# Second attention weights of a two-layer graph kernel: rests by two wide VectorE instructions a group, last load of x moved behind POOL's first group

## Chip, cores and metric

The kernel runs on one core of a Trainium2 chip. The metric is the device time of one execution in microseconds (us). The engines are PE (TensorE), DVE (VectorE), ACT (ScalarE), POOL (GpSimd) and SP (SyncE, which here only issues transfers).

## What is computed

The inputs are x (4096 nodes, D = 128), a weighted adjacency matrix adj (4096 x 4096) and small weights. Two layers follow each other, each added to its input:

```python
h = jnp.maximum(_layernorm(x, axis=-1), 0.0)
x = x + _L0_gnn_ref(h, adj, L0_gnn_weight, L0_gnn_bias)      # adj @ x_tangent, between norms
h = jnp.maximum(_layernorm(x, axis=-1), 0.0)
x = x + _L1_gnn_ref(h, L1_gnn_context, adj, ...)             # attention over the edges
# in _L1_gnn_ref:
logits = left[:, None] + right[None, :]
logits = jnp.where(logits >= 0, logits, 0.2 * logits)
logits = jnp.where(adj_tensor <= 0.0, -jnp.inf, logits)
coefs = jax.nn.softmax(logits, axis=-1)
return jax.nn.relu(coefs @ relation)                         # relation is h
```

A logit is a sum of a row's and a column's number, bent at zero. So the exponential of it is a product of a factor of the row and a factor of the column, with one pair of factors where the sum is negative (weights 0) and one where it is positive (weights 1). The kernel multiplies two matrices of zeros and ones (edge and negative sum, edge and positive sum) with h scaled by the columns' factors, s0 and s1.

## The kernel before, in words

**Tiling.** The 4096 rows stand in NC = 8 chunks of CH = 512 rows; the 4096 columns in NK = 32 blocks k of 128, or NC = 8 groups g of L = 4 blocks. In the first phase (until about 284 us of the trace) adj is loaded chunk by chunk, DVE turns it block by block, PE multiplies it with the tangent vectors (line 715) and ACT keeps the edges as a mask of bytes. In the second phase PE does the attention: for each chunk c and group g it runs 4 row tiles t x 4 blocks k x 2 parts, 32 matmuls of 128 x 258 (line 748, function `attend`).

**What PE multiplies.** `G[0]` and `G[1]` hold for every block k a row of GW = 258 float16 numbers: a head (h times the factor, rounded to float16), a rest (the float32 product less the head, again float16), and the factor itself as two numbers. `G[1]` is written by ACT and DVE, `G[0]` by POOL:
- ACT, `heads(g)` (line 902): four activations write the four heads of `G[1]`, each adding 1 to `head_ready`.
- DVE, `rests(g)` (line 1233): four scalar_tensor_tensor of 128 x 128, each h2 times the column `s1_col`, less the head; each adds 1 to `rest_ready`.
- POOL, the loop of lines 616 to 633: for group g three wide tensor_tensor of 128 x 512, the product with `s0_col` in float32 (line 624), the same product as a float16 head (line 625), and the rest (line 628), which adds 1 to `rest0_ready`. The float32 product is written over the h2 rows of group g - 1, so from group 1 on POOL first waits until `rest_ready` is at 4 g. Before the first group POOL waits for `weight_cols` (DVE, line 1226).

All this is done once, while chunk 0 of the attention runs. For each chunk and group DVE and ACT also make the two matrices of zeros and ones: `compare` (line 1184, two of a group's four blocks by DVE, in chunk 0's group 0 all four), ACT's signs (line 918, the other two), `part_neg` (line 1200) and `part_pos` (line 1207), which adds 1 to `parts_ready`. They have four slots, so the signs and compares of group g wait until PE has used group g - 4.

**Order of the work.** Each engine has its queue written out by hand. In chunk 0 DVE's is, for g = 0 to 7: `part_neg(g)`, `compare(g + 1)`, `rests(g)`, `part_pos(g)` (those of group 0 and the compare of group 1 stand ahead of the loop), with what is left of the first layer's last chunk in between: two sums (lines 1134 and 1138) behind group 0, and statistics (lines 1144 to 1151) behind group 3. POOL also carries pieces of the first layer's last chunk between its groups: `shrink` behind group 1 (lines 558 to 562), which ACT's tanh (line 838) waits for, ahead of its heads of group 3 and its signs of group 3; `residual` (lines 569 to 573) and `store_x1` behind group 2; `affine` behind group 4. PE starts group g of chunk 0 when `parts_ready` is at g + 1, `rest_ready` at 4 g + 4 and `rest0_ready` at g + 1.

**The loads of x.** `load_x(p)` (lines 591 to 596) is four POOL transfers that bring chunk p of x into the buffer `xk`, behind a wait for `h2_ready` at p (ACT has read `xk` for chunk p - 1). Before, the last one, `load_x(7)`, ends the loop of the first layer, ahead of POOL's first group; `residual(7)` reads what it brings.

Of the kernel before, what the change touches and what calls it, by code (L numbers as in the profile page):

```python
# [34 lines left out]
F32 = mybir.dt.float32  # L35
# [5 lines left out]
ALU = mybir.AluOpType  # L41
# [4 lines left out]
P = 128  # L46
Q = 32
NQ = P // Q
L = 4
CH = L * P  # L50
# [36 lines left out]
def bass_two_graph_layers(nc, x, adj, weight, bias, context, w_common, w_left, b_left, w_right, b_right, out):  # L87
# [8 lines left out]
    with ExitStack() as ctx:  # L96
# [3 lines left out]
        def sem(name):  # L100
            return ctx.enter_context(nc.semaphore(name))
# [22 lines left out]
        def view(tensor, offset, shape, dt):  # L124

            size = {F32: 4, F16: 2, I32: 4, I8: 1, F8: 1}[dt]
            n = 1
            for s in shape:
                n *= s
            v = tensor[:, offset:offset + n * size].bitcast(dt)  # L130
            if len(shape) == 2:
                v = v.rearrange("p (a b) -> p a b", a=shape[0])
            if len(shape) == 3:
                v = v.rearrange("p (a b c) -> p a b c", a=shape[0], b=shape[1])
            return v
# [21 lines left out]
        def halves_of(dt, shape):  # L157

            n = L * CH
            return ([view(room, at * slot_bytes + half * n, shape, dt) for at in range(SLOTS)] for half in (0, 1))  # L160
        signs_of, _ = halves_of(I8, [L, CH])
        neg_words, pos_words = halves_of(I32, [L * CH // 4])
        neg, pos = halves_of(F8, [L, CH])
# [56 lines left out]
        def late(shape):  # L220
# [55 lines left out]
        nl_loaded = [sem("nl_loaded_even"), sem("nl_loaded_odd")]  # L276
        weight_cols = sem("weight_cols")
        head_ready, rest_ready, rest0_ready = sem("head_ready"), sem("rest_ready"), sem("rest0_ready")
        edges_ready, signs_ready, compared, coded = (sem("edges_ready"), sem("signs_ready"), sem("compared"),
                                                     sem("coded"))  # L280
        parts_ready, parts_used = sem("parts_ready"), sem("parts_used")
# [80 lines left out]
        def four(g):  # L362

            return slice(g * L, (g + 1) * L)
# [76 lines left out]
        def _(pool):  # L441
# [163 lines left out]
            for p in range(NC - 1):  # L605
                shrink(p)
                residual(p)
                store_x1(p)
                beside(BESIDE_FIRST + 2 * p + 0)
                if p == NC - 2:  # L610
                    scaled_weights()
                affine(p)
                beside(BESIDE_FIRST + 2 * p + 1)
                load_x(p + 1)

            pool.wait_ge(weight_cols, 1)
            for g in range(NC):
                ks, place_of = (slice(n * L, n * L + L) for n in (g, (g - 1) % NC))
                scaled, head, rest = h2[:, place_of, :], G[0][:, ks, 0:D], G[0][:, ks, D:2 * D]
                pool.wait_ge(h2_ready, g + 1)  # L620
                if g:
                    pool.wait_ge(rest_ready, g * L)
                weight_0 = s0_col[:, ks].unsqueeze(2).broadcast_to([P, L, D])
                nc.gpsimd.tensor_tensor(scaled, h2[:, ks, :], weight_0, ALU.mult).then_inc(rest0_scaled, 1)  # L624
                nc.gpsimd.tensor_tensor(head, h2[:, ks, :], weight_0, ALU.mult).then_inc(head0_ready, 1)
                pool.wait_ge(rest0_scaled, g + 1)
                pool.wait_ge(head0_ready, g + 1)
                nc.gpsimd.tensor_tensor(rest, scaled, head, ALU.subtract).then_inc(rest0_ready, 1)  # L628
                if g == 1:
                    shrink(NC - 1)  # L630
                if g == 2:
                    residual(NC - 1)
                    store_x1(NC - 1)
                if g == 4:
                    affine(NC - 1)
# [310 lines left out]
        def _(dve):  # L946
# [280 lines left out]
            ins.then_inc(weight_cols, 1)  # L1227
            last.pop(0)()

            def rests(g):  # L1230
                for k in range(g * L, g * L + L):
                    dve.wait_ge(head_ready, k + 1)
                    v.scalar_tensor_tensor(out=G[1][:, k, D:2 * D], in0=h2[:, k, :], scalar=s1_col[:, k:k + 1],  # L1233
                                           in1=G[1][:, k, 0:D], op0=ALU.mult, op1=ALU.subtract).then_inc(
                        rest_ready, 1)

            def split(c, parity):
                number = isinstance(c, int)
                first = number and c == 0
                if not first:  # L1240
                    dve.wait_ge(nl_loaded[parity], nl_count(c, parity))
                    compare(c, parity, 0)
                for g in range(NC):
                    if not (first and g == 0):
                        part_neg(c, g)
                    if g + 1 < NC and not (first and g == 0):
                        compare(c, parity, g + 1)
                    if first:
                        rests(g)
                    if not (first and g == 0):  # L1250
                        part_pos(c, g)
                    if first:
                        for _ in range({0: 2, 3: 3}.get(g, 0)):
                            last.pop(0)()
                    if g == (0 if number and c == 1 else 1) and not first:
                        take_rows(c - 1)
# [65 lines left out]
```

## Time and profile before

| what | value |
|---|---|
| median of 3 runs (lowest to highest) | 549.21 us (549.14 to 549.24) |
| the profiled execution, its time | 548.11 us |
| its span, first to last instruction | 546.3 us |
| mean granted TensorE clock | 0.968 |
| PE busy | 475.9 us, 87% |
| DVE busy | 449.3 us, 82% |
| ACT busy | 314.5 us, 58% |
| POOL busy | 271.1 us, 50% |

The profiled execution lies 1.10 us under the median of the runs, and its span 1.8 us under its own time; what lies around the span is the launch and the end. Start and length in the timeline and the chain are in us from the span's start. In an idle time in brackets the arrow names what ended it. An instruction's record begins when it is handed to the engine and can hold time in which the engine waits for a resource; records of one engine overlap a little.

### The profile page before, as it was taken

What the parts mean: (1) busy time and instruction counts of PE and PEld (TensorE: products, weight loads), DVE (VectorE), ACT (ScalarE), POOL (GpSimd) and SP (SyncE); (2) the same over time, 40 slices, a digit from 0 to 9 for tenths busy, and PEclk for the clock granted to TensorE, in tenths of its full rate; (3) what the DMA queues carried; (4) which work ended last, traced back from release to release, by engine and by line L of the source; (5) the groups of instructions that cost most, each with busy time, mean ns of one, the idle gap of its engine ahead of it and who ended that gap; (6) DMA issues with size and microseconds to landing.
All of it is one profiled execution on the core that took longest, in us unless ns stands there. A gap on an engine that the chain in (4) does not pass through costs nothing.

```text
span 546.3 us, 9391 instructions
## 1 busy us (share of the span) xinstructions
PE 475.9 (87%) x3209; PEld 412.6 (76%) x3209; DVE 449.3 (82%) x907; ACT 314.5 (58%) x466; POOL 271.1 (50%) x348
## 2 busy tenths in 40 slices
PE   1632879999999999999986387899999999999994
PEld 1532758888888888888864266688888888888884
DVE  3997878888888888888988899968787878878763
ACT  1684776787777777777765633336253535353521
POOL 6850799897969696463649994102020202020200
PEclk9985999999999999999997999899999999999998
DMA  7999999999999999997930101010101010101010
GB/s 173 191 229 221 235 298 307 288 330 316 337 298 335 310 331 311 328 304 194 276 90 22 38 1 40 19 40 20 40 20 40 20 40 17 43 9 32 1 40 20
DMA packets 91851, 84.75 MB, mean 155 GB/s; under 512 B 7552, under 2 KB 89728, under 8 KB 91808
## 3 DMA queue, kind: packets, MB, share of 16 engines
q1 hardware_dynamic: 56032, 48.64, 35.2%
q10 hardware_dynamic: 33424, 31.20, 20.4%
q0 software_dynamic: 2352, 4.35, 2.8%
q8 instruction: 25, 0.41, 0.3%
q14 instruction: 18, 0.15, 0.1%
HBM read 79.96 MB, written 4.21 MB: 154 GB/s over the span
## 4 chain that ended last, share of the span: by engine, by line
PE 74%; DVE 15%; DMA 4%; POOL 2%; issue 2%; ACT 2%; ACTq 0%; SPq 0%; POOLq 0%; DVEq 0%
PE ps L715 37%; PE ps L748 35%; DMA room<-in_adj_dram 3%; DVE room L1233 2%; DVE room L1200 2%; DVE room L1184 1%; DVE room L1207 1%; DVE mask L956 1%; DVE room L998 1%; DVE mask L1010 1%; DVE mask L1006 1%; DMA mask<-in_x_dram 1%; DVE mask L1016 1%; PE ps L702 1%; POOL h_room L624 0%
## 5 line engine op out<-in xcount | busy, mean ns | idle before, releaser
L748 PE MATMUL ps<-room 128*128 128x258 f16 x2048 | 231.8, 276 | 22.7 <-POOL room L628 15.8
L715 PE MATMUL ps<-room 128*128 128x256 f32 x1024 | 225.5, 381 | 22.9 <-DVE room L1116 22.9
L748 PEld LDWEIGHTS ps<-room 128*128 128x128 fp8e4 x2048 | 200.4, 98 | 54.1 <-issue 16.5
L715 PEld LDWEIGHTS ps<-room 128*128 128x128 f32 x1024 | 194.5, 191 | 51.5 <-DVE room L998 17.6
L870 ACT ACTIVATE mask<-room,constants 128x1024 int8<-128x1024 f32 x128 | 146.6, 1146 | 57.8 <-DVE room L998 55.1
L998 DVE STREAM_TRANSPOSE room<-room 128x512 f32<-128x512 f32 x184 | 126.3, 701 | 18.6 <-PE ps L715 13.5
L642 POOL TENSOR_TENSOR h_room<-h_room 128x512 f32<-128x512 f32 x7 | 8.9, 1273 | 148.0 <-DVE post L1274 148.0
L1200 DVE SCALAR_TENSOR_TENSOR room<-mask,constants,room 128x512 int32<-128x512 int32 x64 | 64.4, 1006 | 10.5 <-ACT room L918 10.4
L918 ACT ACTIVATE room<-relu_u,r_col 128x512 int8<-128x512 f32 x64 | 42.0, 713 | 42.3 <-PE ps L748 42.3
L918 ACT ACTIVATE room<-room,r_col 128x512 int8<-128x512 f32 x62 | 40.9, 712 | 32.9 <-PE ps L748 32.8
L998 DVE STREAM_TRANSPOSE room<-mask 128x512 f32<-128x512 f32 x72 | 49.9, 702 | 7.3 <-PE ps L715 6.3
L1207 DVE SCALAR_TENSOR_TENSOR room<-mask,constants,room 128x512 int32<-128x512 int32 x64 | 48.5, 758 | 0.3
L492 POOL TENSOR_TENSOR mask<-mask,h_room 128x2048 f32<-128x2048 f32 x8 | 36.4, 4552 | 23.1 <-DMA mask<-in_L_gnn_context_dram 22.8
L501 POOL TENSOR_TENSOR mask<-mask 128x1024 f32<-128x1024 f32 (+6 forms) x56 | 44.9, 803 | 4.1
L1184 DVE TENSOR_SCALAR room<-room,r_col 128x512 int8<-128x512 f32 x66 | 36.8, 601 | 9.3 <-PE ps L748 9.3
L939 ACT ACTIVATE h_room<-ps,factors 128x258 f32<-128x258 f32 x32 | 15.2, 476 | 49.2 <-PE ps L748 48.2
L1184 DVE TENSOR_SCALAR room<-relu_u,r_col 128x512 int8<-128x512 f32 x64 | 32.2, 544 | 11.5 <-PE ps L748 11.5
L1263 DVE SCALAR_TENSOR_TENSOR h_room<-ps,factors,h_room 128x258 f32<-128x258 f32 x32 | 15.3, 485 | 16.8 <-ACT h_room L939 16.1
L596 POOL DMA_DIRECT2D xk<-in_x_dram x32 | 18.0, 568 | 4.3 <-ACT h_room L847 2.9
L589 POOL DMA_DIRECT2D out_dram<-xk x32 | 18.3, 582 | 2.4 <-POOL xk L573 2.4
L847 ACT ACTIVATE h_room<-xk,post 128x128 f32<-128x128 f32 x32 | 13.1, 479 | 10.6 <-POOL post L582 10.6
L1233 DVE SCALAR_TENSOR_TENSOR room<-h_room,factors,room 128x128 f16<-128x128 f32 x32 | 16.7, 579 | 0.0
(160 smaller groups left out, 339.2 us busy)
## 6 DMA issues: line engine op xcount, KB each, us to landing
room<-in_adj_dram SPq DMA_DIRECT2D x100, 256.0 KB, 7.4
room<-in_adj_dram ACTq DMA_DIRECT2D x84, 256.0 KB, 8.9
mask<-in_adj_dram SPq DMA_DIRECT2D x40, 256.0 KB, 7.4
mask<-in_adj_dram ACTq DMA_DIRECT2D x32, 256.0 KB, 9.0
mask<-in_L_gnn_context_dram SPq DMA_DIRECT2D x16, 256.0 KB, 11.4
xk<-in_x_dram POOLq DMA_DIRECT2D x32, 64.0 KB, 6.2
out_dram<-xk POOLq DMA_DIRECT2D x32, 64.0 KB, 5.5
h_room<-out_dram SPq DMA_DIRECT2D x32, 64.0 KB, 2.5
```

The costliest lines, as they stand in the source:

```text
L492: side(tt(room_of, cx[:, ks, :], v_rows[:, w, :].unsqueeze(1).broadcast_to([P, BESIDE, C]), ALU.mult))
L501: side(tt(dst, room_of[:, :, 0:n], room_of[:, :, n:2 * n], ALU.add))
L589: pool.dma_start(out_n[p, b], xk[b * Q:(b + 1) * Q]).then_inc(x1_stored, 16)
L715: mm = pe.matmul(acc[parity][:, h], xt[:, tangent_order.index(blocks_of(c, k)[j]), :], turned[:, k % TSLOTS, j * (CH // 2):(j + 1) * (CH / ...
L748: mm = pe.matmul(ps[:, 2 * t + w, 0:GW], part[slot(c, g)][:, kk, t * P:(t + 1) * P], G[w][:, k, :], start=(k == 0), stop=(k == NK - 1))
L870: nc.scalar.activation(mc[:, l, h, s:s + L], turned[:, slots:slots + HB, :].rearrange("p s (j i) -> p (s j) i", j=2), ACT.Sign, bias=const ...
L918: ins = nc.scalar.activation(signs_of[slot(c, g)][:, kk, :], nl[parity], ACT.Sign, scale=-1.0, bias=r_col[:, k:k + 1])
L998: v.transpose(turned[:, k % TSLOTS, :].rearrange("p (j r i) -> p j r i", j=2, r=RH), loaded[slot_of[c * NC + g]][:, :, 2 * l * Q:2 * (l + ...
L1184: ins = v.tensor_scalar(signs_of[slot(c, g)][:, kk, :], nl[parity], r_col[:, k:k + 1], -1.0, ALU.is_gt, ALU.mult)
L1200: v.scalar_tensor_tensor(out=neg_words[n], in0=edges_of(c, g), scalar=ones, in1=neg_words[n], op0=ALU.bitwise_and, op1=ALU.bitwise_and).th ...
L1207: v.scalar_tensor_tensor(out=pos_words[n], in0=edges_of(c, g), scalar=ones, in1=neg_words[n], op0=ALU.bitwise_and, op1=ALU.bitwise_xor).th ...
L1233: v.scalar_tensor_tensor(out=G[1][:, k, D:2 * D], in0=h2[:, k, :], scalar=s1_col[:, k:k + 1], in1=G[1][:, k, 0:D], op0=ALU.mult, op1=ALU.s ...
```

## The change

DVE's four small instructions of a group become two of 128 x 512: a product in float32 into a room of its own (`rest_products`, two of them in turn: free room behind `G`, and `support_T`), issued behind `part_neg(g)` and ahead of `compare(g + 1)`, and a subtraction of the heads, where the four stood. POOL's `load_x(7)` moves behind its group 0.

```diff
+        at = nl_at + 2 * gw_bytes + CH * 4
+        rest_products = [view(room, at, [L, D], F32), support_T.rearrange("p (l d) -> p l d", l=L)]
+        assert at + L * D * 4 <= room.shape[1] - CH * 4
...
+        rest_scaled = sem("rest_scaled")
...
                 beside(BESIDE_FIRST + 2 * p + 1)
-                load_x(p + 1)
+                if p + 1 < NC - 1:
+                    load_x(p + 1)
...
                 nc.gpsimd.tensor_tensor(rest, scaled, head, ALU.subtract).then_inc(rest0_ready, 1)
+                if g == 0:
+                    load_x(NC - 1)
...
+            def scale_rests(g):
+                dve.wait_ge(head_ready, g * L + 1)
+                if g >= 2:
+                    dve.wait_ge(rest_ready, (g - 1) * L)
+                v.tensor_tensor(rest_products[g % 2], h2[:, four(g), :],
+                                s1_col[:, four(g)].unsqueeze(2).broadcast_to([P, L, D]), ALU.mult).then_inc(
+                    rest_scaled, 1)
+
             def rests(g):
-                for k in range(g * L, g * L + L):
-                    dve.wait_ge(head_ready, k + 1)
-                    v.scalar_tensor_tensor(out=G[1][:, k, D:2 * D], in0=h2[:, k, :], scalar=s1_col[:, k:k + 1],
-                                           in1=G[1][:, k, 0:D], op0=ALU.mult, op1=ALU.subtract).then_inc(
-                        rest_ready, 1)
+                dve.wait_ge(head_ready, g * L + L)
+                dve.wait_ge(rest_scaled, g + 1)
+                v.tensor_tensor(G[1][:, four(g), D:2 * D], rest_products[g % 2], G[1][:, four(g), 0:D],
+                                ALU.subtract).then_inc(rest_ready, L)
...
                     if not (first and g == 0):
                         part_neg(c, g)
+                    if first:
+                        scale_rests(g)
```

## Rows read from the trace of the kernel before

**Rows 1.** The page: the span, and each engine's busy time and share

```profile
span 546.3 us, 9391 instructions
...
PE 475.9 (87%) x3209; PEld 412.6 (76%) x3209; DVE 449.3 (82%) x907; ACT 314.5 (58%) x466; POOL 271.1 (50%) x348
```

**Rows 2.** Stretches: busy us of PE, PEld, DVE, ACT, POOL; granted clock, DMA share, GB/s

```profile
286.00:302.00 16.00, 9.16 (x64) 7.10 (x64) 12.90 (x26) 9.59 (x26) 14.88 (x17) 0.79 0.06 18
302.00:318.00 16.00, 8.11 (x59) 6.44 (x60) 15.96 (x25) 7.16 (x18) 14.71 (x19) 0.89 0.12 33
318.00:334.00 16.00, 11.64 (x103) 9.53 (x100) 16.00 (x23) 5.37 (x12) 13.23 (x11) 1.00 0.00 1
```

**Rows 3.** The chain that ended last, from 280 us: start, length, what

```profile
299.27 0.21 ACT post L838
...
301.97 1.09 DVE room L1200
...
343.82 56.23 PE ps L748 x494
```

**Rows 4.** Timeline, POOL and TensorE at the start and the end of chunk 0

```profile
286.00 0.43 DVE L1226 TENSOR_TENSOR room<-factors,room 128x32 f16<-128x32 f32 x2
...
286.40 2.24 POOL L596 DMA_DIRECT2D xk<-in_x_dram  x4 [2.85 <-ACT h_room L847]
...
288.65 1.05 POOL L624 TENSOR_TENSOR h_room<-h_room,factors 128x512 f32<-128x512 f32 x1
...
291.91 1.49 POOL L624 TENSOR_TENSOR h_room<-h_room,factors 128x512 f32<-128x512 f32 x1
...
292.11 9.16 PE L748 MATMUL ps<-room 128*128 128x258 f16 x64 [7.13 <-POOL room L628]
...
334.36 7.22 PE L748 MATMUL ps<-room 128*128 128x258 f16 x64 [1.12 <-DVE room L1207]
```

**Rows 5.** Timeline, VectorE in group 2, POOL without a wide instruction

```profile
297.38 0.74 DVE L1200 SCALAR_TENSOR_TENSOR room<-mask,constants,room 128x512 int32<-128x512 int32 x1
298.04 0.87 DVE L1184 TENSOR_SCALAR room<-room,r_col 128x512 int8<-128x512 f32 x2
...
298.83 1.13 DVE L1233 SCALAR_TENSOR_TENSOR room<-h_room,factors,room 128x128 f16<-128x128 f32 x4
...
299.88 0.74 DVE L1207 SCALAR_TENSOR_TENSOR room<-mask,constants,room 128x512 int32<-128x512 int32 x1
```

**Rows 6.** Timeline, VectorE and POOL both with wide instructions, groups 5 and 6

```profile
323.29 1.49 POOL L624 TENSOR_TENSOR h_room<-h_room,factors 128x512 f32<-128x512 f32 x1
323.81 1.52 DVE L1200 SCALAR_TENSOR_TENSOR room<-mask,constants,room 128x512 int32<-128x512 int32 x1
...
324.74 1.48 POOL L625 TENSOR_TENSOR room<-h_room,factors 128x512 f16<-128x512 f32 x1
```

**Rows 7.** Groups by line and form, 283 to 345 us

```profile
L1233 DVE SCALAR_TENSOR_TENSOR room<-h_room,factors,room 128x128 f16<-128x128 f32 x32 | 16.7, 579 | 0.0
...
L624 POOL TENSOR_TENSOR h_room<-h_room,factors 128x512 f32<-128x512 f32 x8 | 10.0, 1246 | 1.6 <-DVE room L1233 1.5
```

**Rows 8.** VectorE tensor_tensor on float32 by form, whole span

```profile
L1293 DVE TENSOR_TENSOR h_room<-h_room 128x256 f32<-128x256 f32 x2 | 0.9, 426 | 0.1
...
L967 DVE TENSOR_TENSOR mask<-mask 128x128 f32<-128x128 f32 x1 | 0.3, 261 | 0.0
```

**Rows 9.** Timeline, VectorE's longest waits and what POOL ran

```profile
304.64 3.02 DVE L1233 SCALAR_TENSOR_TENSOR room<-h_room,factors,room 128x128 f16<-128x128 f32 x4
...
305.98 1.27 POOL L573 TENSOR_TENSOR xk<-relu_u,xk 128x512 f32<-128x512 f32 x1
...
309.44 3.01 DVE L1200 SCALAR_TENSOR_TENSOR room<-mask,constants,room 128x512 int32<-128x512 int32 x1
309.84 1.06 POOL L624 TENSOR_TENSOR h_room<-h_room,factors 128x512 f32<-128x512 f32 x1
310.84 1.05 POOL L625 TENSOR_TENSOR room<-h_room,factors 128x512 f16<-128x512 f32 x1
```

## The prediction, made before the changed kernel was run

> **What bounds the kernel now.** I read the page first: PE is busy 87% and DVE 82% of the span, so either could bound it, and it depends on the stretch [rows 1]. Then the busy time by stretch. From 302 to 334 us, while chunk 0 of the attention runs, DVE is busy 15.96 and 16.00 of 16 us and PE only 8.11 and 11.64 [rows 2]. There DVE sets the pace. From 343.82 us on the chain stays on PE without a break [rows 3], so whatever is won or lost before that point moves the end by as much, and nothing behind it is touched by the change. The point to follow is the start of PE's last group of chunk 0, 334.36 us, released by DVE's `part_pos` [rows 4].
>
> Ahead of 302 us DVE isn't the bound (12.90 of 16 us busy [rows 2]). The chain runs there over POOL: group 0, group 1, `shrink`, then ACT's tanh at 299.27, ACT's signs of group 3, and DVE's `part_neg(3)` at 301.97 [rows 3].
>
> The third reading is what DVE's busy time is made of. The 32 small instructions of line 1233 have a mean of 579 ns, 16.7 us in all, the largest group that the change touches [rows 7]. In group 2, where POOL runs no wide instruction, four of them take 1.13 us, and the next instruction starts 1.05 us after the first [rows 5]. In group 3 the four take 3.02 [rows 9]. So more than half of those 16.7 us is waiting. For what, rows 6 show: POOL's product starts at 323.29 and ends at 324.78; DVE's `part_neg`, handed over at 323.81, ends at 325.33, 0.55 us behind that; the next POOL instruction, handed over at 324.74, ends at 326.22, some 0.9 us behind DVE's. The two engines' instructions take turns, and none begins its work before the other's is done. Alone, DVE's takes 0.74 [rows 5] and POOL's 1.05 [rows 4].
>
> **The change, part by part.** *Executing.* Removed in each group: four small ones, 1.05 us of DVE's queue when nothing is in the way. Added: two tensor_tensor of 128x512. None of this form is in the trace. The nearest are 128x256 at 0.426 and 128x128 at 0.261 [rows 8]; 128 more elements cost 0.165, so 512 cost about 0.426 + 2 x 0.165 = 0.76. The other bound is from 128 elements between the two forms of line 1233 and the wide ones: (0.74 - 0.34) / 3 = 0.13, where 0.34 is 1.13 less three steps of 0.26; this gives 0.69. Records overlap by 0.08 (0.74 long, the next 0.66 later [rows 5]), so a pair takes 1.22 to 1.36 us, 0.17 to 0.31 more than the four.
>
> *Waiting.* It is tempting to say that two instructions wait half as often as four. But in taking turns it is each wide POOL instruction that holds up one DVE instruction, whichever is next: POOL has three a group, 24 in all, and they all have to be done before the last group. The number of waits is POOL's, not DVE's. What falls out of the small ones' waits comes up again in front of `part_neg`, `compare` or `part_pos`. And a small one that waited cost only its last 0.15 us behind POOL's end, a wide one 0.55 [rows 6], so under contention the pair costs about 1.15 against 0.8 for the four with two of them waiting. Per group I take +0.22 us, between 0.17 and 0.35. On the bounded stretch lie groups 3 to 7: 5 x 0.22 = **+1.1 us** (0.9 to 1.75).
>
> *Place in the queue.* The product goes ahead of `compare(g + 1)`. In groups 1 to 6 its end is awaited behind two compares, so the new wait costs nothing there; in groups 0 and 7 the two stand back to back, and the second waits for the first's signal, some 0.1 us, inside the rounding of the term above. ACT's first head of a group precedes its signs, which `part_neg` has waited for, so the wait on `head_ready` is met. POOL's group g + 1 waits for `rest_ready` as before; only in group 7 was that wait felt, 1.5 us [rows 7], and the signal again comes right ahead of `part_pos(6)`. `support_T` is free: PE's transposes have read it before DVE's ReLU, which DVE ran ahead of the loop.
>
> *The load moved.* Its four issues hold POOL for 2.24 us, and group 0 starts at 288.65; without them it could start when DVE's line 1226 is done, 286.43 [rows 4], 2.2 us earlier. Then the issues follow, and group 1 starts behind both. So group 1, on which the chain goes on, gains nothing: 286.45 + 3.3 (three products: the first starts at 288.65, and PE, which the third releases, at 292.11) + 2.24 = 292.0 against 291.91 [rows 4]. But group 0 ran beside sums on DVE that did not hold it up; now DVE's two wide ones of group 0 fall into it, up to 0.55 each, so the start is between 292.0 and 293.1. Some is given back: `part_neg(1)` and a compare then run beside the issues rather than into group 1, whose product took 1.49 instead of 1.05 [rows 4]. The delay of group 1's end is 0 to 0.9 us; it passes through `shrink`, the tanh and the signs to `part_neg(3)`. I take **+0.4**. PE's first group starts about 1.5 us earlier than 292.11, and wins nothing, since its later groups wait for `part_pos` and for POOL's group 2. The data are wanted at 305.98 by `residual` [rows 9], and are issued by some 292.9: with a landing of a few us they are hidden; the cover would be gone only if they came 13 us late, and then each us more would cost one.
>
> Sum: +1.1 + 0.4 = +1.5 us. The profiled execution would take 548.11 + 1.5 = 549.6 us; it lies 1.1 us under the median of the runs, so for the median 549.21 + 1.5 = **550.7 us**, 0.27% more. A measurement of this kernel tells about 0.2%, 1.1 us, from no change.
>
> **A rule against the second part.** The issues of `load_x(6)`'s kind beside small DVE instructions took 2.24 us for four, 0.56 each [rows 4], so they were not held up; now they stand beside compares and wide products. The Trainium skill (SBUF — State Buffer, section SBUF: two separate sides) says that transfers issued by GpSimd starve while VectorE runs in a mode with two ports, because the descriptors can't be written. By that rule the issues would last as long as DVE's compares and wide ones beside them. It is the second rival below.
>
> **Rivals.**
> 1. *The waits do go with the count* (faster). Speaking for it: 16.7 us of small ones of which only 32 x 0.34 = 10.9 is work [rows 7], so 5.8 us waits. If a wait is paid per DVE instruction, groups 3 to 7, which carry nearly all of it, save half: -2.9 + 1.1 = -1.8, 547.4 us. It decides once POOL is so late that its last groups run behind DVE. Against it: POOL's last group waits for DVE [rows 7], so POOL is not the late one. In the same direction goes `part_neg(4)`, 3.01 us, over two POOL instructions at 309.84 and 310.84 instead of one [rows 9]; with other times it may wait for one, -1.5. Chance together 0.26.
> 2. *The issues starve* (slower). Beside them would lie a `part_neg`, a product and two compares, 0.66 + 0.65 + 0.8 = 2.1 us of DVE; all of it on POOL's start of group 1 gives, with the other terms, +3.6: 552.8 us. Chance 0.05.
> 3. *It cancels* (within 0.2%). The first part's cost is there, but `part_neg(4)` waits for one POOL instruction less, or the pair comes at 0.69 and POOL's first groups gain what they lose: 0 to +1, 549.7 us. Chance 0.29.
> 4. The forecast, +1.1 to +2.6, 550.7 us: chance 0.40.
>
> **How the numbers follow.** Slower is 0.40 + 0.05, within 0.2% 0.29, faster 0.26. The range leaves out the outermost part of rival 1 and rival 2: from 547.4, where the halved waits end, to 551.9, which is the upper end of both terms (1.75 + 0.9). The slower case alone reaches from 550.3 to 551.9.
>
> **What would show it.** Right: line 1233's successors at 0.69 to 0.76 where POOL is idle and 1.1 to 1.6 beside it; `part_neg`, compares and `part_pos` of groups 3 to 7 with a larger mean than before; DVE still busy 16 of 16 us from 302 to 334; PE's last group of chunk 0 at about 335.9 instead of 334.36; the tanh at 299.3 to 300.2. Wrong: DVE idle in that stretch, waiting for POOL or ACT; the PE group at 333 or earlier; the four issues of line 596 above 0.7 us each.

## The result, and the profile after

Twenty runs of each kernel: 551.38 us against 549.52 us, a ratio of 1.004 with a 95% interval of 1.0022 to 1.0059. By the ratio the change makes the kernel slower by 1.2 to 3.2 us, 2.2 in the middle; the medians differ by 1.9. The forecast was 550.7, slower by 1.5. The profiled execution took 549.02 us, 0.9 more than the one of before. That difference alone would mislead, as the stretches below show.

The twenty times of the changed kernel fall into two groups: eleven lie at 548.6 to 551.4 us (middle 549.75) and nine at 553.2 to 555.7. None of the twenty of before lies above 552.0. Both traces of the changed kernel (549.02 and 548.78 us) are of its lower group; no trace shows what the upper one does.

The page of the changed kernel:

```profile
span 547.2 us, 9389 instructions
...
PE 478.5 (87%) x3209; PEld 414.1 (76%) x3209; DVE 451.6 (83%) x891; ACT 314.4 (57%) x466; POOL 274.7 (50%) x348
```

Its stretches, with the columns named in the first line:

```profile
core 0: us, PE busy (x) PEld busy (x) DVE busy (x) ACT busy (x) POOL busy (x), PEclk, DMA share, GB/s
286.00:302.00 16.00, 8.80 (x64) 6.75 (x64) 15.33 (x22) 8.03 (x23) 14.10 (x15) 0.79 0.06 18
302.00:318.00 16.00, 7.55 (x39) 5.32 (x40) 13.66 (x21) 9.48 (x24) 15.01 (x17) 0.69 0.11 33
318.00:334.00 16.00, 13.90 (x109) 11.13 (x107) 15.88 (x15) 5.38 (x12) 15.25 (x14) 0.89 0.00 1
```

Against [rows 2], DVE is busier ahead of 302 us (15.33 for 12.90), and from 302 to 318 us it is no longer always busy: 13.66 of 16 us. That is not relief. It is a wait at the beginning of the stretch, for ACT's signs, which follow the tanh. The chain (start, length, what), and the row of `part_neg(3)` from the timeline:

```profile
301.60 0.20 ACT post L845
...
346.38 53.68 PE ps L755 x486
```

```profile
304.29 0.93 DVE L1207 SCALAR_TENSOR_TENSOR room<-mask,constants,room 128x512 int32<-128x512 int32 x1 [2.79 <-ACT room L925]
```

The tanh comes at 301.60 instead of 299.27, `part_neg(3)` at 304.29 instead of 301.97, and PE goes on without a break from 346.38 instead of 343.82 [rows 3]. POOL and PE in the timeline:

```profile
287.26 1.04 POOL L629 TENSOR_TENSOR h_room<-h_room,factors 128x512 f32<-128x512 f32 x1 [2.97 <-DVE room L1233]
...
288.25 1.49 POOL L630 TENSOR_TENSOR room<-h_room,factors 128x512 f16<-128x512 f32 x1
...
291.21 2.24 POOL L600 DMA_DIRECT2D xk<-in_x_dram  x4
...
293.47 1.05 POOL L629 TENSOR_TENSOR h_room<-h_room,factors 128x512 f32<-128x512 f32 x1
...
332.04 3.68 PE L755 MATMUL ps<-room 128*128 128x258 f16 x32 [0.48 <-POOL room L633]
...
336.91 7.22 PE L755 MATMUL ps<-room 128*128 128x258 f16 x64 [1.19 <-DVE room L1214]
```

POOL's group 0 starts 0.1 us behind DVE's weight columns (287.18, the end of line 1233 now), its second product takes 1.49 because DVE's wide instruction comes between, and behind the four issues group 1 starts at 293.47. PE's last group of chunk 0 starts at 336.91, again released by `part_pos`; before 334.36 [rows 4].

**Measuring from marks of the kernel's own.** Single traces start this part at different times: the weight columns were done at 286.43 us before and 287.18 after, and 289.85 in one run of an experiment, though nothing ahead of them differs. So all kernels are compared by stretches, each read from timeline rows: *start* from the end of the weight columns to POOL's first product of group 0, *to shrink* from the weight columns to POOL's first small step of `shrink`, *shrink* from there to the end of the step that releases the tanh, *A* from the weight columns to the tanh, *B* from the tanh to PE's last group of chunk 0, *C* from there to the end.

| kernel | start | to shrink | shrink | A | B | A + B | C |
|---|---|---|---|---|---|---|---|
| before | 2.22 | 9.50 | 3.30 | 12.84 | 35.09 | 47.93 | 211.95 |
| before, again | 1.87 | 8.98 | 3.43 | 12.44 | 35.34 | 47.78 | 211.95 |
| after | 0.08 | 9.88 | 4.51 | 14.42 | 35.32 | 49.74 | 210.28 |
| after, again | 0.08 | 9.94 | 4.50 | 14.48 | 35.32 | 49.80 | 210.31 |
| wide only | 2.76 | 10.32 | 4.50 | 14.85 | 35.32 | 50.17 | 210.29 |
| load only | 0.08 | 9.37 | 3.30 | 12.71 | 35.05 | 47.76 | 210.28 |
| product twice | 0.08 | 10.42 | 5.84 | 16.30 | 39.70 | 56.00 | 210.27 |
| load by SP | 0.08 | 7.49 | 3.82 | 11.35 | 35.36 | 46.71 | 211.95 |
| products by ACT | 2.21 | 9.60 | 4.24 | 13.87 | 33.86 | 47.73 | 211.80 |
| wide from group 3 | 1.88 | 8.98 | 3.43 | 12.45 | 35.74 | 48.19 | 210.28 |
| wide below group 3 | 2.76 | 10.33 | 4.50 | 14.86 | 34.91 | 49.77 | 210.29 |
| statistics later | 2.72 | 10.00 | 3.30 | 13.33 | 34.39 | 47.72 | 210.28 |
| SP and statistics | 0.08 | 7.49 | 3.82 | 11.35 | 34.66 | 46.01 | 210.28 |
| ACT from group 3 | 0.08 | 7.49 | 3.83 | 11.35 | 34.46 | 45.81 | 211.78 |

A + B went from 47.93 and 47.78 to 49.74 and 49.80: +1.9 us, within 0.15 us both times. The profiled execution of after took only 0.9 us more: its weight columns were done 0.75 us later, A + B is 1.81 longer, and C is 1.67 shorter. Both traces of before have the longer C and both of after the shorter; experiments that change nothing behind the last group have the one or the other. Nearly all of the 1.9 lies in A (+1.6 between the first traces, +2.0 between the second), and there the largest part in `shrink` (+1.2 and +1.1).

The middle of the changed kernel's lower group lies only 0.2 us over the median of before. That would be 1.9 us more in A + B and 1.67 less in C, if the traced C were that of most runs. It needn't be: load only was traced with the shorter C as well, and its median is that of before. The rest of the difference of the medians is the upper group, some 4 us higher. So the 1.9 of the traces and the 1.9 of the medians are not shown to be the same 1.9.

A kernel that loads x ahead of POOL's group 0 has a *start* of 1.87 to 2.76 us, also where nothing differs (before 2.22 and 1.87, statistics later 2.72): POOL's load waits there for ACT (line 847). Where kernels differ in it, the stretch from POOL's start to the tanh, A less *start* and less the 2.24 us of issues where these stand behind group 0, is the better measure. It is 10.6 us in both traces of before and 12.1 in both of after.

**The two new instructions**, by form, 283 to 347 us:

```profile
L1241 DVE TENSOR_TENSOR room<-h_room,factors 128x512 f32<-128x512 f32 x8 | 10.4, 1297 | 0.0
L1248 DVE TENSOR_TENSOR room<-room 128x512 f16<-128x512 f32 x8 | 10.2, 1280 | 0.3
```

The pair was busy 20.6 us in the eight groups, the 32 small ones 16.7 [rows 7]. Beside POOL's wide ones or its issues a wide one takes 1.2 to 1.6 us; without, four times, it takes 0.68.

### The profile page after: what moved, and what is told of

Read it like the earlier page. It is cut to its first block, busy times and chain, and to the rows that moved or that the text cites. A ratio compares the mean times of both kernels' runs of the same rounds, so it can differ in the third digit from the quotient of the medians.

```text
span 547.2 us, 9389 instructions
## 1 busy us (share of the span) xinstructions
PE 478.5 (87%) x3209; PEld 414.1 (76%) x3209; DVE 451.6 (83%) x891; ACT 314.4 (57%) x466; POOL 274.7 (50%) x348
## 3 DMA queue, kind: packets, MB, share of 16 engines
q1 hardware_dynamic: 56032, 48.64, 35.1%
## 4 chain that ended last, share of the span: by engine, by line
PE 73%; DVE 16%; ACT 3%; issue 3%; POOL 3%; DMA 1%; ACTq 1%; DVEq 0%; POOLq 0%
PE ps L722 37%; PE ps L755 35%; DVE room L1005 2%; DVE room L1214 2%; DVE room L1191 1%; ACT mask L877 1%; DVE room L1207 1%; DVE room L1241 1%; DVE mask L963 1%; DVE mask L1017 1%; DMA mask<-in_x_dram 1%; DVE mask L1013 1%; DVE room L1123 1%; DVE mask L1023 1%; ACT ps L819 1%
## 5 line engine op out<-in xcount | busy, mean ns | idle before, releaser
L1123 DVE SCALAR_TENSOR_TENSOR room<-mask,ps 128x128 f32<-128x128 f32 x32 | 9.7, 340 | 7.5 <-ACT ps L819 7.5
```

## The experiments

**Wide only, load only.** The two parts of the change by themselves.

```diff
 # e1_wide_only, against the changed kernel
-                if p + 1 < NC - 1:
-                    load_x(p + 1)
+                load_x(p + 1)
...
-                if g == 0:
-                    load_x(NC - 1)
```

> The changed kernel with the last load of x at its old place ahead of POOL's first group; only the two wide instructions are left of the change. Two stretches are read: A, from the end of DVE's weight columns (line 1226 before) to ACT's tanh, 12.84 us before and 14.42 us with both parts; B, from the tanh to PE's last group of chunk 0, 35.09 us before and 35.32 us with both parts. Theory (the wide instructions hold up POOL's small steps of shrink, which took 3.3 us before and 4.5 us with both parts): A stays long, 13.6 to 14.2 us, although the load is back; B 35.3 to 36.2; time 1.0 to 2.0 us over the kernel before. Rival (the moved load made A long): A 12.8 to 13.0, and the time is within 0.5 us of the kernel before or longer only by what B shows.

```diff
 # e2_load_only, against the kernel before
-                load_x(p + 1)
+                if p + 1 < NC - 1:
+                    load_x(p + 1)
...
+                if g == 0:
+                    load_x(NC - 1)
```

> The kernel before with its last load of x moved behind POOL's group 0; the four small instructions stay. Theory: group 0 starts 2.2 us earlier and group 1 within 0.3 us of its old place, so A is 12.8 to 13.3 us, B 35.0 to 35.3, the time within 0.5 us of the kernel before. Rival (the moved load is what delays the tanh, through group 0 falling beside DVE's instructions or issues held up by DVE's compares): A 13.8 to 14.4, four issues longer than 0.6 us each, time 1.0 to 1.6 us more.

Wide only: 551.65 us against 548.98, ratio 1.006 (1.004 to 1.0081). Load only: 548.97 against 548.98, ratio 0.9996 (0.998 to 1.0012). Both rivals fell, and both theories held in kind, not in every size: wide only came out above its ranges, with A 14.85 for 13.6 to 14.2 and 2.7 us more time for 1.0 to 2.0, and load only with A 12.71 just under 12.8. The cost is the wide instructions' alone. The moved load is worth nothing that shows: the start of group 0 gains 2.1 us (2.22 to 0.08), and the issues behind it take them back before `shrink` (9.50 to 9.37; the second trace of before has 8.98). Wide only shows A even longer than the full change, 14.85; 0.5 us of that is its later start of POOL (2.76 for 2.22), which stands ahead of anything the wide ones touch. Less that start it is 12.1 us, as in the full change. The group of long times goes with the pair as well: two of the six runs of wide only lie at 553.7 us, and none of load only above 551.1.

**What makes shrink long.** The steps of `shrink` ahead of the tanh, on POOL before the change:

```profile
295.93 0.25 POOL L558 TENSOR_SCALAR post<-post 128x8 f32<-128x8 f32 x1
296.26 1.80 POOL L559 TENSOR_TENSOR post<-post,powers 128x8 f32<-128x8 f32 x1
...
298.15 0.80 POOL L560 TENSOR_SCALAR post<-post 128x4 f32<-128x4 f32 x1
...
299.03 0.20 POOL L561 TENSOR_TENSOR post<-post 128x4 f32<-128x4 f32 x1
```

and after it, with three of DVE's instructions beside them:

```profile
295.92 1.60 DVE L1248 TENSOR_TENSOR room<-room 128x512 f16<-128x512 f32 x1
297.06 0.57 POOL L562 TENSOR_SCALAR post<-post 128x8 f32<-128x8 f32 x1
...
297.71 2.18 POOL L563 TENSOR_TENSOR post<-post,powers 128x8 f32<-128x8 f32 x1
...
299.98 0.97 POOL L564 TENSOR_SCALAR post<-post 128x4 f32<-128x4 f32 x1
300.16 0.68 DVE L1248 TENSOR_TENSOR room<-room 128x512 f16<-128x512 f32 x1
300.76 0.74 DVE L1214 SCALAR_TENSOR_TENSOR room<-mask,constants,room 128x512 int32<-128x512 int32 x1
301.03 0.54 POOL L565 TENSOR_TENSOR post<-post 128x4 f32<-128x4 f32 x1
```

Each of POOL's small steps is longer: 0.57 for 0.25, 2.18 for 1.80, 0.97 for 0.80, 0.54 for 0.20. The first was handed over while the wide subtraction of group 1 (295.92) was at work, and ended 0.11 us behind it. The step at 301.03 was handed over while `part_pos(2)` (300.76) was at work, and ended 0.07 us behind it. `part_pos(2)` is in both kernels; the pair only changed where it falls. Taking turns works in both directions: a step of 0.2 us waits until a DVE instruction of some 0.7 us is done. Two kernels put the wide pair on one side of the tanh each:

```diff
 # e6_wide_from_3 (wide = (3, 4, 5, 6, 7)) and e7_wide_below_3 (wide = (0, 1, 2)),
 # against e1_wide_only
             def rests(g):
+                if g not in wide:
+                    for k in range(g * L, g * L + L):
+                        dve.wait_ge(head_ready, k + 1)
+                        v.scalar_tensor_tensor(out=G[1][:, k, D:2 * D], in0=h2[:, k, :], scalar=s1_col[:, k:k + 1],
+                                               in1=G[1][:, k, 0:D], op0=ALU.mult, op1=ALU.subtract).then_inc(
+                            rest_ready, 1)
+                    return
...
-                    if first:
+                    if first and g in wide:
                         scale_rests(g)
```

> The last load of x at its old place, the two wide instructions in groups 3 to 7 only, four small ones in groups 0 to 2. Theory (the wide ones of groups 1 and 2 make shrink long): shrink 3.2 to 3.5, A 12.6 to 13.4; B 35.3 if part_neg(4) is free, up to 37 if it waits for two POOL instructions; time from 0 to 2 us over the kernel before. Rival (shrink is long for another reason): shrink 4.5, A 14.4 or more.

> The last load of x at its old place, the two wide instructions in groups 0 to 2 only, four small ones from group 3 on. Theory: shrink 4.4 to 4.6, A 14.0 to 14.9; B as before, 35.1 with the double wait of part_neg(4) or 33.6 without it; time 0 to 2 us over the kernel before. Rival: A 12.8, and B alone carries what the change costs.

Small ones below group 3 bring `shrink` back to 3.43 and A to 12.45; wide ones there alone make it 4.50 and A 14.86. Of these 2.4 us in A 0.88 is POOL's start (1.88 against 2.76), which the edits don't reach; the other 1.5 are the pair's, 1.07 in `shrink` and 0.46 ahead of it. The steps with small ones below group 3:

```profile
295.56 0.30 POOL L562 TENSOR_SCALAR post<-post 128x8 f32<-128x8 f32 x1
...
295.94 1.67 POOL L563 TENSOR_TENSOR post<-post,powers 128x8 f32<-128x8 f32 x1
...
297.69 0.88 POOL L564 TENSOR_SCALAR post<-post 128x4 f32<-128x4 f32 x1
...
298.66 0.33 POOL L565 TENSOR_TENSOR post<-post 128x4 f32<-128x4 f32 x1
```

So the larger part of the loss in A + B is settled: A takes it, mostly through `shrink`, from the wide pairs of groups 0 to 2. Which of the three groups it is was not separated. Nor are wide instructions needed to lengthen `shrink`: with small ones alone it takes 3.30, 3.43 or, in the kernels with the load by SP, 3.82 us, by where the steps fall among DVE's instructions. A + B is 48.19 and 49.77 us. The times, 549.42 (0.9988 to 1.0017) and 550.42 against 549.02 (0.9992 to 1.0032), can't be told from no change, though their order is the one of A + B. B of e7, 34.91, was expected at 35.1 with the double wait of `part_neg(4)`, and its trace has that wait (3.01 us). B of e6, 35.74, has none. This allows a clean reading of B. The second trace of before and wide from group 3 have the same A (12.44 and 12.45), and so have wide below group 3 and wide only (14.86 and 14.85). In both pairs of kernels the wide ones in groups 3 to 7 add 0.4 us to B (35.34 to 35.74, 34.91 to 35.32), although the double wait goes.

**Do the waits go with DVE's instructions or with POOL's?** One more wide instruction a group:

```diff
 # e3_product_twice, against the changed kernel
+        spare_product = view(room, at + L * D * 4, [L, D], F32)
...
+                v.tensor_tensor(spare_product, h2[:, four(g), :],
+                                s1_col[:, four(g)].unsqueeze(2).broadcast_to([P, L, D]), ALU.mult)
```

> The changed kernel with each group's wide product made twice, the second time into a room that nobody reads; one more wide DVE instruction a group. Theory (DVE and POOL take turns and the number of waits is POOL's): on stretch B it costs its own work, 0.55 to 0.65 us for each of groups 3 to 7, so B is 35.3 + 3.0 = 38.3 (37.8 to 38.8); the time 3.5 to 4.5 us over the changed kernel with what groups 1 and 2 add. Rival (each DVE instruction pays a wait of its own, 0.85 us on top): B 35.3 + 7 = 42.3 us.

B grew by 4.4 us, to 39.70: between the two and outside the theory's 37.8 to 38.8, but nearer to its 3.0 than to the 7 of the rival. A grew by 1.9, with `shrink` at 5.84, so A + B is 6.3 us over the changed kernel, where 3.5 to 4.5 were expected. Its trace shows where the rest can lie: `part_neg(4)` is back at a double wait, which the changed kernel's trace doesn't have.

```profile
314.24 2.87 DVE L1208 SCALAR_TENSOR_TENSOR room<-mask,constants,room 128x512 int32<-128x512 int32 x1
314.51 1.06 POOL L630 TENSOR_TENSOR h_room<-h_room,factors 128x512 f32<-128x512 f32 x1
...
315.51 1.05 POOL L631 TENSOR_TENSOR room<-h_room,factors 128x512 f16<-128x512 f32 x1
```

In the changed kernel the same instruction starts 0.9 us ahead of POOL's group 3 and is free, and so is the product behind it:

```profile
311.78 0.72 DVE L1207 SCALAR_TENSOR_TENSOR room<-mask,constants,room 128x512 int32<-128x512 int32 x1
312.42 0.68 DVE L1241 TENSOR_TENSOR room<-h_room,factors 128x512 f32<-128x512 f32 x1
312.71 1.29 POOL L629 TENSOR_TENSOR h_room<-h_room,factors 128x512 f32<-128x512 f32 x1
313.02 2.44 DVE L1191 TENSOR_SCALAR room<-room,r_col 128x512 int8<-128x512 f32 x2
```

So the rival that prices a wait per DVE instruction is ruled out in the size it needs; that the theory is exact to 0.1 us isn't shown. The time was 555.93 against 548.98, ratio 1.0131.

**Is the double wait worth having away?** The kernel before, with the statistics behind `part_neg(4)`:

```diff
 # e8_stats_later, against the kernel before
                         part_neg(c, g)
+                    if first and g == 4:
+                        while last:
+                            last.pop(0)()
...
-                        for _ in range({0: 2, 3: 3}.get(g, 0)):
+                        for _ in range({0: 2}.get(g, 0)):
```

> The kernel before with one step moved: the statistics of the last chunk of x (lines 1144 to 1151) run behind part_neg(4) on DVE instead of ahead of it. Theory (part_neg(4), handed over 0.4 us ahead of POOL's group 3, is held up by two POOL instructions, and isn't where it comes earlier, as in the changed kernel): part_neg(4) takes 0.74 us instead of 3.01, B falls from 35.09 to 33.3 to 33.8, time 1.2 to 1.8 us under the kernel before. Rival (the waits are POOL's count and turn up elsewhere): part_neg(4) short, but the compares and rests(4) behind it longer by as much, B 34.8 to 35.2, no difference in time.

```profile
308.93 0.74 DVE L1200 SCALAR_TENSOR_TENSOR room<-mask,constants,room 128x512 int32<-128x512 int32 x1
...
310.53 1.06 POOL L624 TENSOR_TENSOR h_room<-h_room,factors 128x512 f32<-128x512 f32 x1
...
310.78 3.35 DVE L1184 TENSOR_SCALAR room<-room,r_col 128x512 int8<-128x512 f32 x2
311.53 1.05 POOL L625 TENSOR_TENSOR room<-h_room,factors 128x512 f16<-128x512 f32 x1
```

`part_neg(4)` takes 0.74, as expected, but the first of the two compares now waits through both POOL products instead (2.09 us; the two take 3.35). B falls by 0.7 us (35.09 to 34.39), half of the theory's 1.5 and not the rival's zero: part of the wait came up again one instruction later. A + B falls by 0.2 only, since POOL's start came 0.5 us later in this trace (2.72 for 2.22). The load by SP without and with the same edit (below) has one A, 11.35, and there too B falls by 0.70 (35.36 to 34.66). The time is 547.74 against 549.02, ratio 0.9975 (0.9958 to 0.9992).

**Taking work from POOL and from DVE.** The last load of x issued by SP:

```diff
 # e4_load_by_sp, against the kernel before (last_xk_loaded is a new semaphore)
+            sp.wait_ge(x1_stored, (NC - 1) * (16 * NQ))
+            sp.wait_ge(h2_ready, NC - 1)
+            for b in range(NQ):
+                sp.dma_start(xk[b * Q:(b + 1) * Q], x_n[NC - 1, b]).then_inc(last_xk_loaded, 16)
             sp.wait_ge(x1_ready, NC)
...
-                load_x(p + 1)
+                if p + 1 < NC - 1:
+                    load_x(p + 1)
```

> The kernel before with its last load of x issued by SP, which is idle there, instead of POOL (with a semaphore of its own); the four small instructions stay. Theory: POOL's group 0 starts when the weight columns are done, 2.2 us earlier, and nothing is put between groups 0 and 1, so the tanh comes 1.5 to 2.2 us earlier (A 10.6 to 11.3 us) and PE's last group of chunk 0 as much; time 547.0 to 547.9 us against 549.5. Rival (DVE's queue and not POOL's sets when group 3 starts, or PE's clock takes it back): A falls but B grows by the same, the time is within 0.5 us of the kernel before.

A fell by 1.5 to 11.35, B grew by 0.3; together 1.2 us less. A was expected at 10.6 to 11.3. The start moved by 2.1 us, so a third was lost on the way: POOL's group 0 now meets DVE's rests, and `shrink` took 3.82. The time, 548.09 against 548.98, ratio 0.9997 (0.9981 to 1.0013), doesn't show the 1.2 us: theory and rival can't be told apart by it, though the stretch speaks for most of the theory.

ACT makes the float32 products, and DVE keeps one wide subtraction a group:

```diff
 # e5_act_products, against e1_wide_only (DVE's scale_rests is gone)
+            def products(g):
+                if g >= 2:
+                    act.wait_ge(rest_ready, (g - 1) * L)
+                for k in range(g * L, g * L + L):
+                    nc.scalar.activation(rest_products[g % 2][:, k - g * L, :], h2[:, k, :], ACT.Copy,
+                                         scale=s1_col[:, k:k + 1]).then_inc(rest_scaled, 1)
...
+                    if number and c == 0:
+                        products(g)
...
-                dve.wait_ge(rest_scaled, g + 1)
+                dve.wait_ge(rest_scaled, g * L + L)
```

> The last load of x at its old place, and ACT makes the float32 products (four activations a group behind its signs); DVE has one wide subtraction a group left. Stretches as before: A from the weight columns to the tanh (12.84 us before, 14.42 with both parts, 14.85 with the wide instructions alone), B from the tanh to PE's last group of chunk 0 (35.09, 35.32, 35.32), shrink from POOL's first small step to the one ahead of the tanh (3.30, 4.51, 4.50). Theory (turns: POOL's waits stay, each wide instruction less saves its own work of 0.6 us): B 32.3 to 33.8, the upper end if part_neg(4) waits for two POOL instructions; shrink 3.3 to 3.9, A 12.8 to 13.9; time 1.5 to 3 us under the kernel before. Rival (ACT becomes the bound with 1.2 us more a group, 3.6 us in all against some 5.5 of DVE): part_neg waits for ACT's signs in groups 4 to 7, B 35 or more, no gain.

B is 33.86, 1.5 us under that of the pair, just outside what was expected, and without a double wait of `part_neg(4)`. The 3.0 us of work saved aren't all seen: PE's last two groups of chunk 0 are released by POOL's third instruction here (line 632, after waits of 0.73 and 0.48 us), no longer by `part_pos`. `shrink` stays long with one wide instruction a group, 4.24, so A is 13.87 and A + B, 47.73, is no better than before. Nor is the time, of which 1.5 to 3 us less were expected: 548.5 against 549.02, 0.9988 (0.9972 to 1.0004).

The last two kernels put together what shortened a stretch:

```diff
 # e9_sp_and_stats: e4_load_by_sp with the edit of e8_stats_later.
 # e10_act_from_3: e9, with products by ACT and one wide subtraction from group 3 on, small ones below.
+                    if number and c == 0 and g >= 3:
+                        products(g)
```

> The kernel before (four small instructions) with both steps that shortened a stretch: the last load of x by SP, and the statistics behind part_neg(4). The start of POOL's group 0 to the tanh took 10.62 us before; the stretch from the weight columns to PE's last group of chunk 0 took 47.93 us before, 46.71 with the load by SP alone, 47.72 with the statistics moved alone. Theory (the gains add): 45.6 to 46.4 us, time 1.5 to 2.3 us under the kernel before. Rival (what is won on POOL ahead of the tanh is lost behind it, since DVE then meets POOL's groups at other places): 46.7 or more, at most 1.2 us under.

> As e9, and from group 3 on ACT makes the float32 products and DVE has one wide subtraction a group; groups 0 to 2 keep the four small ones, so that shrink isn't held up. Theory (a small group costs DVE 0.8 to 1.05 us, the one wide 0.55 to 0.6, the waits are POOL's): 0.25 to 0.45 us less in each of groups 3 to 7 than e9, so 43.8 to 45.0 us from the weight columns to PE's last group, shrink 3.3 to 3.9 us, time 2.5 to 4 us under the kernel before. Rival (ACT's four more instructions a group make part_neg wait): no better than e9.

e9: A + B 46.01, which is 47.93 less the 1.22 of the load by SP and the 0.70 that the statistics' move takes from B; 546.87 us against 549.34, ratio 0.9954 (0.9936 to 0.9971). e10: 45.81 instead of 43.8 to 45.0, so the theory's size was wrong; 546.3 us, ratio 0.994 (0.9916 to 0.9964). Its PE rows tell why. The last groups of chunk 0 are released by POOL's third instruction of a group (line 641 there) and no longer by `part_pos`:

```profile
330.67 3.68 PE L761 MATMUL ps<-room 128*128 128x258 f16 x32 [0.73 <-POOL room L641]
...
334.56 7.21 PE L761 MATMUL ps<-room 128*128 128x258 f16 x64 [0.21 <-POOL room L641]
```

Once DVE has less to do, POOL's three instructions a group are the bound, and work taken from DVE bought 0.2 us more. Both kernels beat the two of this case; which of them is the better is not settled.

**The same kernels once more.**

> The kernel before once more, unchanged. From one run to the next its time differs by some 4 us; the question is which stretches that lies in. Theory: the stretch from the weight columns to PE's last group of chunk 0 is set by the order of the instructions and comes out at 47.8 to 48.3 us again; what differs lies ahead of it (the first layer's end at 284.7 us in the first trace, up to 287.7 in others) and behind it (211.95 or 210.28 us, by the clock granted to TensorE as it goes on after its last pause). Rival: that stretch itself differs by 1 us or more.

> The changed kernel once more, unchanged. Theory: the stretch from the weight columns to PE's last group of chunk 0 comes out at 49.5 to 50.0 us again, 1.6 to 2.0 over the kernel before, whatever the time of the run. Rival: it lies anywhere between 48 and 51 and the difference to the kernel before isn't the change's.

549.31 and 550.29 us, against 548.92 in the same rounds (ratios 1.0013, 0.9995 to 1.0031, and 1.0029, 1.0002 to 1.0057). A + B came out at 47.78 and 49.80, each within 0.15 us of its first trace. For this stretch the rival of a chance difference falls. Two of the ten times of the changed kernel lie above 552 us again (552.87 and 553.51), and none of before's.

## Why the prediction was right, point by point

The direction was right and the size near: 1.5 us against 2.2 by the ratio and 1.9 by A + B. But the two terms of the sum were not the two that were measured: +1.1 on B and +0.4 on A were forecast, +0.2 and +1.6 came (0.0 and +2.0 between the second traces). That the sum is near is luck: one error made up for the other. It is luck too that the medians agree with A + B, as C and the untraced upper group of runs stand between them.

- *What bounds.* PE's last group of chunk 0 was released by `part_pos` before and after, and the shift of that point, by its distance from the weight columns, is the loss. But DVE no longer sets the pace alone. POOL's wait for DVE in group 7, 1.5 us before [rows 7], is gone, and PE's group ahead of the last is released by POOL's third instruction (332.04, after 0.48 us).
- *Executing* (+1.1 on B). The pair's own time was read well: 0.68 us each when free, against 0.69 to 0.76. B grew by only 0.23 in the profiled executions, and by 0.4 in the two pairs of kernels with the same A. The rest of the term is offset by the double wait of `part_neg(4)`, 3.01 us before and 0.72 after, which the prediction had left where it was in its sum. The statistics' move prices that wait at 0.7 us of B, so the term itself comes out near 0.4 + 0.7 = +1.1, an estimate, and what was forecast. This is an inference from several kernels, not a measurement of the term alone: a trace with the double wait and the pair in groups 3 to 7, the rest as in the changed kernel, is missing.
- *Waiting.* That waits don't halve with the count: B grew, and did not fall by the 1.8 us of rival 1; the third wide instruction cost 0.9 us a group (4.4 / 5), not 1.4. The listed sign, a larger mean of `part_neg`, compares and `part_pos` in groups 3 to 7, came only in part: `part_neg` went from 1.58 to 1.10 us and the compares from 0.96 to 0.84, `part_pos` from 0.92 to 1.43. Together they took 20.1 us before and 19.4 after; without `part_neg(4)` it is 17.1 and 18.6. The rests themselves went from 12.4 to 13.6.
- *The load moved* (+0.4 on A). Two statements here. That group 1 would end 0 to 0.9 us later was right in sum: 9.50 to 9.88 us until `shrink`. That the moved load was the cause was wrong: load only came out at 9.37, nothing, and the delay was the wide pair's beside POOL's groups 0 and 1. The mis-sized term is this one, +0.4 for a measured +1.6 to +2.0, and the failing step is the one after: "The delay of group 1's end is 0 to 0.9 us; it passes through `shrink`, the tanh and the signs". `shrink` was taken as a fixed length. It grew by 1.2 us, the largest single item of the loss, because POOL's small steps wait for DVE's longer instructions and for those that the pair moved beside them. The prediction looked at POOL holding up DVE and not at DVE holding up POOL in a place where POOL was the chain.
- *Rivals.* Rival 1's own mechanism fell; its rider, that `part_neg(4)` might wait for one POOL instruction less, came true and was worth 0.7 us of B, half of its 1.5. Rival 2 fell: the four issues took 2.24 us after as before, beside `part_neg` and a wide product. What the Trainium skill says of such issues (SBUF — State Buffer, section SBUF: two separate sides) doesn't appear in these traces. They are a weak test of it, since it speaks of a mode with two ports, no compare stood beside the issues (the next one was handed over at 293.52, behind them), and no row tells an instruction's mode. What the same section says of the pair of ports, that it is held for the whole of an instruction and the other engine waits, fits the small steps: 0.54 us for a step of 0.20.
- *What would show it.* The last group was foretold at 335.9 and came at 336.91, of which 0.75 is the later start; the tanh came at 301.60 or, less that, 300.85, outside 299.3 to 300.2. DVE was idle in the stretch, 2.79 us in front of `part_neg(3)` and waiting for ACT, where before it was 1.35. That was listed as a sign that the forecast is wrong, and it did point at what was wrong in it: the chain over POOL and ACT was late, by more than the term on A allowed.

## What to carry to other kernels

Where two engines take turns at a resource, a longer instruction can cost twice: its own work on its engine, and the wait of the small steps of the other engine that fall beside it. Ask for each stretch which of the two is the chain: where it is the engine with the small steps (`shrink`), four short instructions were better neighbours here than two long ones (3.3 to 3.8 us against 4.5), and merging is only worth trying where the merged engine bounds and the other has slack. And measure a change of 2 us between two marks inside the kernel: A + B repeated within 0.15 us, where whole runs spread over 5 to 7. But what lies outside the marks has to be traced as well: C took back 1.67 us, and a trace of a run in the upper group is what this case lacks.

## What was not expected of the hardware

A DVE instruction can wait through two POOL products that follow each other, where elsewhere it comes between them. It was seen where POOL had just issued transfers or stood at its first product behind them: `part_neg(4)` at 3.01 us in both traces of before, 2.87 with the product twice, a compare in e8. Small ones do it too: in the second trace of before the fourth of group 0's four, handed over at 288.61 during the issues, took 2.87 us, and 0.34 in the first. It isn't there where the DVE instruction was handed over 0.9 us ahead of POOL's product. POOL's issues seem to hold up DVE's wide ones as well, though not always. In the changed kernel:

```profile
291.21 2.24 POOL L600 DMA_DIRECT2D xk<-in_x_dram  x4
...
291.41 0.73 DVE L1207 SCALAR_TENSOR_TENSOR room<-mask,constants,room 128x512 int32<-128x512 int32 x1
292.07 1.52 DVE L1241 TENSOR_TENSOR room<-h_room,factors 128x512 f32<-128x512 f32 x1
```

The wide product of group 1 takes 1.52 us beside the third and fourth issue, with no POOL product begun before 293.47, and 1.53 in the second trace of the same kernel; `part_neg(1)`, beside the first two, takes 0.73, and a wide product beside the last issue of `store_x1`, at 312.42, takes 0.68. Which part of an issue does it is open.

The stretch C had two lengths. It took 211.78 to 211.95 us in five traces (both of before, load by SP, and the two with products by ACT) and 210.27 to 210.31 in the other nine. TensorE's granted clock was 0.58 from 344 to 348 us before, where it goes on after its last pause (line 748 at 343.82), so most of that time at the lower of its two levels, 1.2 GHz, and 1.00 (2.4 GHz) from 344 to 352 us in the changed kernel's trace, where it goes on at 346.38. The pause ahead of it was 2.25 us in both. Why one goes on slowly and the other doesn't is open, and so is whether it goes with the kernel; it is worth 1.67 us, about as much as the change.
